# Causal attention with the scores' sign turned: Relu in PSUM and a select on GpSimd for most mask products, V copied by ScalarE

## What is computed

```python
qkv = hidden_states @ w_attn + b_attn
q, k, v = jnp.split(qkv, 3, axis=-1)                 # 32 heads of 16
scores = jnp.einsum('bqhd,bkhd->bhqk', q, k) * SCALE
bias = slopes[:, None, None] * rel[None, :, :]       # rel = key position - query position
scores = jnp.where(rel <= 0, scores + bias, -jnp.inf)
attn = jax.nn.softmax(scores, axis=-1)
out = jnp.einsum('bhqk,bkhd->bqhd', attn, v)
return out @ w_proj + b_proj
```

## Time and profile before

| | |
|---|---|
| median of 3 runs | 920.68 us (920.47 to 921.09) |
| the profiled execution | 918.81 us, its span 917.0 us |
| granted TensorE clock, mean | 0.98 |
| start of the attention loop, end of its last product with V | 428.25 us, 680.15 us |
| busy shares over the span | PE 94%, DVE 82%, ACT 48%, POOL 29% |

### The profile page before, as it was taken

How to read it: one execution, slowest core, us unless ns; L and a number is a source line. 1 busy time by engine, 2 the same in 40 slices (tenths; PEclk the granted TensorE clock), 3 DMA queues, 4 the chain that set the end, 5 groups by cost and what they waited for, 6 DMA issues and landing times.

```text
span 917.0 us, 12232 instructions
## 1 busy us (share of the span) xinstructions
PE 857.6 (94%) x4223; PEld 411.2 (45%) x4223; DVE 755.7 (82%) x1621; ACT 439.2 (48%) x800; POOL 261.9 (29%) x214
## 2 busy tenths in 40 slices
PE   6998978999989999999999999999999999999996
PEld 3444424454446444444444444444434444444442
DVE  5799999999998866889989998996146799766877
ACT  4767644666642031102666667667533655433100
POOL 1068999899974000050000000000000343000000
PEclk9889999999999999999999999999999999999998
DMA  9200060200005026401122202200033000000001
GB/s 346 104 0 1 1 275 27 112 1 0 1 4 202 0 81 199 158 18 40 51 79 79 60 23 78 81 3 2 1 132 116 0 1 0 0 1 0 12 36 45
DMA packets 22136, 54.34 MB, mean 59 GB/s; under 512 B 5957, under 2 KB 12741, under 8 KB 19066
## 3 DMA queue, kind: packets, MB, share of 16 engines
q1 hardware_dynamic: 22074, 53.56, 17.0%
HBM read 44.96 MB, written 8.39 MB: 58 GB/s over the span
## 4 chain that ended last, share of the span: by engine, by line
PE 60%; DVE 7%; SPq 2%; issue 1%; DMA 1%; ACT 1%; POOL 0%; POOLq 0%; DVEq 0%
PE ps L1197 16%; PE ps L1059 8%; PE ps L1208 6%; PE ps L1041 6%; PE ps L1028 4%; PE ps L1025 3%; PE ps L1118 3%; PE ps L970 3%; PE ps L1098 3%; PE ps L1081 2%; SPq L316 2%; PE ps L1044 2%; DVE ps L1469 1%; PE ps L779 1%; DVE mrow L1473 1%
## 5 line engine op out<-in xcount | busy, mean ns | idle before, releaser
L732 ACT ACTIVATE prob<-ps 128x512 f32<-128x512 f32 x288 | 160.0, 599 | 126.4 <-PE ps L1044 98.1
L477 POOL TENSOR_TENSOR hC<-hs,C_sb 128x512 f32<-128x512 f32 x128 | 160.2, 1268 | 50.8 <-ACT C_sb L672 31.1
L950 PE MATMUL ps<-hC,identf 128*128 128x512 f32 x256 | 136.8, 634 | 15.0 <-POOL hC L477 13.6
L1041 PE MATMUL ps<-stack 123*128 123x512 bf16 (+3 forms) x384 | 113.8, 327 | 0.2
L601 ACT ACTIVATE ps<-dtT,nA 128x512 f32<-128x512 f32 x128 | 88.2, 690 | 49.8 <-DVE hs L1352 46.5
L431 POOL TENSOR_TENSOR rstd<-veps,mhalf 128x4 f32<-128x4 f32 x8 | 8.5, 1067 | 353.4 <-DVE veps L1235 353.4
L1476 DVE TENSOR_REDUCE mrow<-ps 128x1 f32<-128x512 f32 x128 | 81.8, 684 | 10.0 <-PE ps L1028 9.7
L1059 PE MATMUL ps<-prob,V 128*32 128x512 f32 (+3 forms) x768 | 81.6, 498 | 0.7 <-ACT prob L732 0.7
L1197 PE MATMUL ps<-hT,wg 128*128 128x512 f32 (+1 forms) x176 | 79.1, 592 | 0.0
L1197 PE MATMUL ps<-hT,wu 128*128 128x512 f32 (+1 forms) x176 | 79.1, 592 | 0.0
L950 PEld LDWEIGHTS ps<-hC,identf 128*128 128x128 f32 x256 | 46.3, 197 | 72.9 <-POOL hC L477 56.6
(11 more groups left out here) (199 smaller groups left out, 1329.1 us busy)
## 6 DMA issues: line engine op xcount, KB each, us to landing
stack<-parts_dram SPq DMA_DIRECT2D x96, 128.0 KB
wmod<-in_wmod SPq DMA_DIRECT2D x4, 1536.0 KB, 11.1
parts_dram<-qkp SPq DMA_DIRECT2D x16, 384.0 KB, 2.6
wmod<-in_wmod SPq DMA_DIRECT2D x4, 1024.0 KB, 11.3
wattn<-in_wattn SPq DMA_DIRECT2D x1, 3072.0 KB, 11.4
wg<-in_wg SPq DMA_DIRECT2D x1, 2752.0 KB, 11.2
wu<-in_wu SPq DMA_DIRECT2D x1, 2752.0 KB, 9.4
wd<-in_wd SPq DMA_DIRECT2D x1, 2560.0 KB, 11.0
```

What stands on the lines that cost most here:

```text
L477: pool.tensor_tensor(hC[:, c, :], hs[:, c, :], C_sb[:, m % 2, :], ALU.mult).then_inc(S["hc_done"], 1)
L732: A_(prob[:, u % 4, j, :], ps[:, 3 + F % 3, :], ACT.Exp).then_inc(S["exp_done"], 1)
L950: mm(ps[:, c, :], identf[:], hC[:, c, :], start=False, stop=(s == NS - 1), skip_group_check=True).then_inc(S["sum_done"], 1)
L1041: ins = mm(ps[:, bank, col:col + w], qk[0:ATT_ALL, 1, j, tile(kb)], qk[0:ATT_ALL, 0, j, q0:q0 + w], start=True, stop=not diag)
```

## The change

- The queries' scale, their bias, the distance bias and the mask constant change sign, so a score is now the negative of what it was. DVE takes minima in place of maxima with the same instructions; the second product gives maximum minus score, which is zero or more where the mask lets it through, and the exponential is taken with scale -1.
- In units 1, 3 and 8 (PAIRS) both mask products go. ACT first applies Relu in place in PSUM to the two diagonal squares (256 of the 512 columns), waits for it, and takes the exponential. Above the diagonal that leaves a number of at most 1. GpSimd then writes zeros there (`affine_select` on `prob`), and PE waits for that (`masked`) ahead of the product with V.
- The product with V comes 7 slots after a unit's first slot, not 6; the copies, turns and divisions that follow it move by one slot (one of them, `normalise(g, 0)`, by two).
- V is copied out of PSUM by ACT, without its bias. The bias is added by DVE to the turned output (`turned`), where it is a number per partition; the weights of a softmax sum to one. Its load shrinks from 128x512 to 128x4.

```diff
+PV_LAG = 7
+PAIRS = tuple(tuple(col // P for kb, q0, w, col in pieces if q0 == kb * P) if len(pieces) == 2 else () for pieces in UNITS)
...
+            for F in range(NG * FU):
+                U, j = F // GH, F % GH
+                on = PAIRS[U % NU]
+                if on:
+                    pool.wait_ge(S["exp_done"], F + 1)
+                    w = prob[:, U % 4, j, :].rearrange("p (n c) -> p n c", c=P)[:, on[0]:on[1] + 1:on[1] - on[0], :]
+                    pool.affine_select(w, w, [[0, 2], [1, P]], ALU.is_ge, 0.0, base=0, channel_multiplier=-1) \
+                        .then_inc(S["masked"], 1)
...
-                   scale=1.0 / HD if ob < DC else 1.0).then_inc(S["qk_evac"], 1)
+                   scale=-1.0 / HD if ob < DC else 1.0).then_inc(S["qk_evac"], 1)
+
+            for t in range(NT):
+                act.wait_ge(S["v_mm"], t + 1)
+                A_(V[:, t, :, 0:HD], ps[:, 4 + t % 4, :].rearrange("p (h d) -> p h d", d=HD), ACT.Copy).then_inc(S["v_done"], 1)
...
-                A_(prob[:, u % 4, j, :], ps[:, 3 + F % 3, :], ACT.Exp).then_inc(S["exp_done"], 1)
-                if g and f == 4:
+                on = PAIRS[u % NU]
+                if on:
+                    x = ps[:, 3 + F % 3, :].rearrange("p (n c) -> p n c", c=P)[:, on[0]:on[1] + 1:on[1] - on[0], :]
+                    bounded = sum(map(bool, PAIRS[0:u % NU])) * GH + j + 1 + g * N_PAIRS * GH
+                    A_(x, x, ACT.Relu).then_inc(S["bounded"], 1)
+                    act.wait_ge(S["bounded"], bounded)
+                A_(prob[:, u % 4, j, :], ps[:, 3 + F % 3, :], ACT.Exp, scale=-1.0).then_inc(S["exp_done"], 1)
+                if g and f == 5:
                     evacuate(g - 1, 1)
-                if f == 20:
+                if f == 21:
                     evacuate(g, 0)
...
-                    diag = q0 == kb * P
+                    diag = q0 == kb * P and not PAIRS[u]
...
                     pe.wait_ge(S["exp_done"], GH * (U + 1))
+                    if PAIRS[u]:
+                        pe.wait_ge(S["masked"], GH * (g * N_PAIRS + sum(map(bool, PAIRS[0:u + 1]))))
...
-                U, j = F // GH - 1, F % GH
+                U, piece = (F - PV_LAG) // GH, (F - PV_LAG) % GH
...
-                if U >= 0 and 0 <= j - 2 < len(UNITS[U % NU]):
-                    weighted_values(U, j - 2)
-                if g and f == 8:
+                if U >= 0 and piece < len(UNITS[U % NU]):
+                    weighted_values(U, piece)
+                if g and f == 9:
                     back(g - 1, 1)
-                if f == 24 and g < NG - 1:
+                if f == 25 and g < NG - 1:
                     back(g, 0)
...
-            def value(t):
-                v.wait_ge(S["v_mm"], t + 1)
-                tt(V[:, t, :, 0:HD], ps[:, 4 + t % 4, :].rearrange("p (h d) -> p h d", d=HD),
-                   vbc[:].rearrange("p (h d) -> p h d", d=HD), ALU.add).then_inc(S["v_done"], 1)
...
-                v.tensor_copy(AOT[:, c, half(h)], ps[:, bank, :]).then_inc(S["aot_evac"], 1)
+                ts(AOT[:, c, half(h)], ps[:, bank, :], bv[:, c:c + 1], None, ALU.add).then_inc(S["aot_evac"], 1)
```

More of the change, by code:

```diff
@@ L35 @@
 LEAD = 12
+PV_LAG = 7
 MAGIC = 12582912.0
-LOW = -3e38
+HIGH = 3e38
 TERMS = ((0, 0), (1, 0), (2, 0), (0, 1), (1, 1), (0, 2))
@@ L69 @@
 NU = len(UNITS)
+PAIRS = tuple(tuple(col // P for kb, q0, w, col in pieces if q0 == kb * P) if len(pieces) == 2 else () for pieces in UNITS)
+N_PAIRS = sum(map(bool, PAIRS))
 FU = NU * GH
@@ L134, in program @@
         Dp = tiny("Dp", [P, DC])
+        bv = tiny("bv", [P, DC])
         bqk = tiny("bqk", [P, 8])
@@ L361, in _ @@
             sp.wait_ge(S["ln_tr"], 3 * NT)
-            load(vbc[:], a["b_v"].partition_broadcast(P), S["bias1"])
+            load(bv[:], a["b_v"], S["bias1"])
             load(bpc[:], a["b_proj"].partition_broadcast(P), S["bias1"])
@@ L1139, in last_group @@
                     project(t, k)
-                if f == 22:
+                if f == 23:
                     back(NG - 1, 0)
-                if f == 25:
+                if f == 26:
                     pe.wait_ge(S["ao_done"], 2 * NG - 1)
@@ L1282, in _ @@
             v.wait_ge(S["in_misc"], 16 * 5)
-            ts(bqk[:, 0:4], bqk[:, 0:4], 1.0 / HD, None, ALU.mult).then_inc(S["negA"], 1)
+            ts(bqk[:, 0:4], bqk[:, 0:4], -1.0 / HD, None, ALU.mult).then_inc(S["negA"], 1)
             ts(nA[:], nA[:], -1.0, None, ALU.mult).then_inc(S["negA"], 1)
@@ L1468, in maximum @@
                     for j_ in range(GH):
-                        ins = v.tensor_tensor_reduce(ps[:, bank, tile(j_)], ps[:, bank, tile(j_)], negT[:], 1.0, LOW,
-                                                     ALU.add, ALU.max, mrow[:, kb, j_, i:i + 1])
+                        ins = v.tensor_tensor_reduce(ps[:, bank, tile(j_)], ps[:, bank, tile(j_)], negT[:], 1.0, HIGH,
+                                                     ALU.add, ALU.min, mrow[:, kb, j_, i:i + 1])
                     ins.then_inc(S["m_done"], 1)
                 elif j is None:
-                    v.reduce_max(mrow[:, kb, :, i], ps[:, bank, :].rearrange("p (j c) -> p j c", c=P), AX) \
+                    v.tensor_reduce(mrow[:, kb, :, i], ps[:, bank, :].rearrange("p (j c) -> p j c", c=P), AX, ALU.min) \
                         .then_inc(S["m_done"], 1)
                 else:
-                    v.reduce_max(mrow[:, 0, j, i:i + 1], ps[:, bank, :], AX).then_inc(S["m_done"], 1)
+                    v.tensor_reduce(mrow[:, 0, j, i:i + 1], ps[:, bank, :], AX, ALU.min).then_inc(S["m_done"], 1)
                 g = n // SU
@@ L1481, in maximum @@
                         v.wait_ge(S["rt_mm"], g)
[L1482 removed]
+                    v.tensor_reduce(rr[:], mrow[:].rearrange("p k j i -> p (j i) k"), AX, ALU.min, negate=True) \
                         .then_inc(S["r_rdy"], 1)
@@ L1544, in _ @@
                     split_shift(NG - 1)
-                if g and f == 11:
+                if g and f == 12:
                     normalise(g - 1, 1)
-                if f == 27 and g < NG - 1:
+                if f == 29 and g < NG - 1:
                     normalise(g, 0)
@@ L1624, in constants @@
         qconst[3 * b:3 * b + 3, b * P:(b + 1) * P] = 1.0
-        for n, part in enumerate(three(sl[:, None] * (j - (b * P + 64)).astype(np.float32)[None, :])):
+        for n, part in enumerate(three(-sl[:, None] * (j - (b * P + 64)).astype(np.float32)[None, :])):
             alibi[:, :, 3 * b + n, :] = part.reshape(NG, GH, T)
@@ L1629, in constants @@
         "sel": bf16_bits(-np.tile(np.eye(2 * NS), (3, 1))),
-        "negm": bf16_bits(np.where(p[:, None] > p[None, :], -1e38, 0.0)),
+        "negm": bf16_bits(np.where(p[:, None] > p[None, :], 1e38, 0.0)),
         "qconst": bf16_bits(qconst), "kones": bf16_bits(np.ones((ATT_R, T))), "alibi": np.ascontiguousarray(alibi.transpose(0, 2, 1, 3)),
@@ L1661 @@
         wlb=c(g["L0_ffn_B"].transpose(0, 2, 1).reshape(E * R, D)),
-        wattn=c(g["L1_attn_w_attn"][:, order]), b_qk=cols(b_attn[0:2 * D]), b_v=c(b_attn[2 * D:]),
+        wattn=c(g["L1_attn_w_attn"][:, order]), b_qk=cols(b_attn[0:2 * D]), b_v=cols(b_attn[2 * D:]),
         wproj=c(g["L1_attn_w_proj"]), b_proj=c(g["L1_attn_b_proj"]),
```

8 lines of the change are left out of this document (2 added, 6 removed).

## The result

The changed kernel takes **909.28 us** (median of 4 runs, 908.71 to 909.71) beside 920.87 (920.47 to 921.09) for the kernel before on the same chip: a ratio of 0.988, 95% interval 0.9865 to 0.9894. 910.0 was forecast.

A forecast was written before the change was run, and what follows sets the result against it. The attention loop was taken as bound by DVE and PE in alternate phases. Groups -9.3, V -1.7 and the end +0.4 made -10.6: 908.2 us from the profiled 918.81, said as 910.0 for the median; range 902.5 to 922.

The forecast's parts named there:

- Two phases, and where the gain comes from: Attention loop: DVE bounds slots 24 to 3, PE slots 4 to 23; the change gives -1.4 us a group.
- The floor of 28.17: DVE's busy time in a 30.80 us group, taken as untouched by the change; at most 2.63 us to gain.
- Mask products: Removing them saves PE 0.9 us a group in units 1 and 3; unit 8's are worth nothing there.
- Relu: On ACT in units 1, 3, 8: 0.373 us plus a 0.03 gap; ACT's group rises to 25.6 us.
- the Relu at 0.60: Rival: a Relu at the 512-column price adds 1.7 us a group, cancelling the gain: 920 us, chance 0.16.
- Select: On GpSimd: 0.6 us for 256 columns, between 0.3 and 1.7, hidden ahead of units 1's and 3's products with V.
- The 0.1 us to start: Start-up time for a GpSimd select, added to the fill's 0.22 us for the lower bound of 0.3.
- The slow-select rival: PE stands at units 1 and 3, 8d - 7.6 us a group; decides from d = 1.15; 929 to 951 us, chance 0.20.
- V: Entry of the loop: with ACT copying V, PE's 2.12 us stand for DVE mostly goes, -1.7 us.
- PE's only limit becomes that copy: Entry of the loop: PE then waits only for ACT's 0.6 us copy of V, the step behind -1.7 us.
- The end: Last stretch: Relus +1.0 and +0.3, sixteen mask products -0.9, last product with V 0; together +0.4 us.
- The 1.0 for unit 8 of group 6: No scores are left there and ACT sets the pace, so four Relus cost +1.0 us.

The follow-up runs named there:

- experiment 1: Changed kernel with the mask products back in every diagonal unit, no Relu and no select (lag 7 and V on ACT stay): 913.23 us, ratio 0.9927.
- experiment 2: Kernel before with only the lag of 7 and the copies, turns and divisions moved with it: 914.41 us, ratio 0.9937.
- experiment 3: Changed kernel with the product with V back at 6 slots, Relu and select kept: 922.43 us, ratio 1.003.
- experiment 9: Changed kernel with unit 8's masks by products again, units 1 and 3 as changed: 908.64 us, ratio 0.9867.
- experiment 5: Changed kernel with Relu over all 512 columns of the bank in place of 256, same result: 925.65 us, ratio 1.0056.
- experiment 4: Changed kernel with V copied by DVE again at its old places, the bias still added at the end: 909.82 us, ratio 0.9889.
- experiment 8: Changed kernel with the next slot's scores ahead of the product with V in slots 7, 11, 15, 19 and 23: 908.84 us, ratio 0.9872.
- experiment 10: Changed kernel with the copy to OT moved behind unit 1, its turn and division later too: 913.58 us, ratio 0.9917.
- experiment 6: Changed kernel with every select issued twice, the second behind the end of the first: 912.6 us, ratio 0.992.

## Why the prediction was right, and which of its terms were not

- **Two phases, and where the gain comes from.** Right. Per group 29.4 was forecast and 29.22 measured, -1.57 against -1.4. The lag gives 0.76 and the masks 0.83 (experiments 1 and 2). DVE's idle time left is 29.22 - 27.87 = 1.35 (forecast 1.2). The floor of 28.17 was not quite fixed: DVE's busy time fell by 0.30, which fits four stops fewer, as a reduction takes 0.69 us behind a stop and 0.60 in a row. The prediction gave both parts a price each; experiment 3 shows that the masks' share exists only at a lag of 7.
- **Mask products.** 0.9 forecast for units 1 and 3, 0.83 measured with Relu and select against them; unit 8's are worth nothing in a group (experiment 9).
- **Relu.** 0.373 and a gap of 0.03 forecast, 0.377 and 0.03 measured; ACT's group was put at 25.6 and was 24.25 by the window, since the gaps aren't busy time and recorded durations overlap (exponentials of 0.60 us follow each other by 0.49). That TensorE has next to no room for later exponentials was right in kind: the Relu at 0.60 was priced at 1.7 a group and 920, and experiment 5 made it 2.33 and 925.65. The term was short because only units 1 and 3 were counted: of the 2.33, some 0.84 arise at unit 8. The Trainium skill (ScalarE: Activation LUTs, Rules for kernel authors) would have Relu on VectorE; no run here put it there, but with ACT doing it the swap gains 0.83 a group, and the engine to which the rule sends it is busy 27.87 of 29.22.
- **Select.** 0.6 taken between 0.3 and 1.7; it is 0.406 us for 256 columns. Hidden in the groups, as forecast: 0.86 us lie between the last exponentials of units 1 and 3 and their products (0.85 and 0.8 in the prediction). Not hidden at the last product with V, see the end. The 0.1 us to start in the prediction's lower bound came from no row. The estimates from the Trainium skill (GPSIMD Engine Reference, section 3.1) were 0.2 and 2.6: the trace has twice the light loop's and a sixth of the branching one's, so the second rule doesn't fit this instruction. The slow-select rival had the right mechanism and a formula one unit short: it breaks even near 1.0 us a slot, not 1.15, and costs 4.95 at 1.31, not 2.9.
- **V.** Mis-sized. The stand at the entry fell by 1.87 us and the entry came 1.76 earlier, as worked out, but only 1.07 reached the next fold (experiment 4). The step that failed is "PE's only limit becomes that copy": it set the entry, but the fold is set by DVE's list, and DVE was still busy with earlier scores when the first of the loop came. It started on them 1.05 us sooner, not 1.76.
- **The end.** +0.4 forecast, 0.0 measured (285.54 and 285.49 us from the last fold to the end of the span). The swap itself costs the 0.40 forecast (285.09 without it, experiment 1); the term left out is the lag, -0.51 (experiment 2). Inside the 0.40 two errors cancel, which is luck: unit 8's swap costs 1.41 (experiment 9), where +1.0 and half of the -0.9 give 0.55, and units 1 and 3 then give back 1.0, where +0.3 and the other half give 0.15. The 1.0 for unit 8 of group 6 was right; the select in the last product's chain was put at 0, and that product starts 0.62 us behind its last exponential (0.05 before), with the wait of 0.66 for GpSimd. The bias in `turned` made its instruction 0.75 us long in place of 0.69, and TensorE's wait for it ahead of the output projection is 0.8 us in both.
- **From one execution to the medians.** The prediction added the 1.9 us by which the median lay above the profiled execution. By the folds the loop gave 10.4 (forecast 9.3), the entry 1.07 (1.7) and the end 0.05 (-0.4): 11.5, not 10.6, and this is what brought the median 0.7 below the forecast. The errors have both signs (1.1 more won in the loop, 0.6 less at the entry, 0.4 more at the end), so that the total comes this near is partly luck.

What still holds the group at 29.2 above DVE's 27.9 is open in part. DVE's two named waits are 0.69 us; the rest, 0.66, is eleven stops under 0.15 us each, for which the profile names no cause (the prediction took such stops for the pipeline running empty, which nothing shows). Moving work from one side of TensorE's queue to the other (experiment 8) changed which engine waits, and not the group. A variant without the Relu at all wasn't tried.

## What to carry to other kernels

Where two engines alternate as the bound, read waits and prices in the phase: the same edit was worth 0.83 us a group in two units, nothing in the third, and cost 1.4 us in that third unit once the scores had ended. Before giving work to an engine that is half idle, look at the slots in which it would do it and at what stands behind its consumer: ACT had 10 us to spare in a group and none in units 1, 3 and 8. A swap that lengthens a chain may need more distance to its consumer to pay: the same Relu and select made the kernel slower at a distance of 6 slots and faster at 7.

## What the runs showed of the hardware that was not expected

**A clock fall that comes and goes with the same code.** Behind a stand of 2.01 us of TensorE ahead of the loop the granted clock read 0.50 (1.2 of 2.4 GHz) in the changed kernel's execution:

```profile
391.37 0.39 PE L1051 MATMUL ps<-stack 120*128 120x512 bf16 x1 [2.01 <-DVE mrow L1489]
391.59 1.53 PE L1123 MATMUL ps<-wattn,hT 128*128 128x512 f32 x2
...
395.05 0.55 PE L1051 MATMUL ps<-stack 120*128 120x512 bf16 x1
```

and in the execution of the kernel before, where the stand was 2.00 us, the same two microseconds read:

```profile
392.00:394.00 2.00, 2.00 (x7) 0.93 (x7) 2.00 (x4) 0.00 (x0) 1.49 (x2) 1.00 0.01 2
```

Seven of the fourteen profiled executions (the changed kernel and experiments 1 to 4, 8 and 10) showed it (a clock of 0.89 over 385 to 400 us), and the others, which stand there for 2.0 us as well, read 1.00. Experiment 2 showed it and the kernel before didn't, with the same code at this place. It cost 1.68 us: experiment 2 has 25.72 us from the end of the stand to the first fold, the kernel before 24.04. That is as much as a term of the sum, so two single executions of such kernels are compared from a fold on, not from the start.

**A select on GpSimd is short**: 0.41 us for two squares of 128 columns, where the rate of the additions here (1.27 us for 512 columns) would make 0.63, and 0.47 from one to the next that waits for it (523.40 to 523.87 in experiment 6).
